# A vision tower on one core: narrow attention in units of three images, MLP branches by running sums, expert down weights loaded later

## The reference

```python
emb = patches @ W_proj + b_proj + pos                      # 64 x 36 x 192
h = layernorm(emb + attention(emb))                        # attn1: 12 heads of 64, causal
# attn2 and mlp; images 0..31 "large", images 32..63 "small"
a = attn(ln(h), 12 heads of 16)                            # small: sum over i of g[i] * attn with 12/(i+1) heads
x = h + a
mlp(x) = gelu(x @ w_fc1 + b_fc1) @ w_fc2 + b_fc2           # small: sum over i of g[i] * mlp that
                                                           # sees and keeps only 192/(i+1) channels
h = layernorm(h + x + mlp(ln(x)))
h = layernorm(h + attention(h))                            # attn3: 12 heads of 16, distance bias
h = layernorm(h + moe(h))                                  # a shared MLP, and 2 of 8 experts
```

## Time and profile before

| what | value |
|---|---|
| median of three timed runs | 917.89 us |
| profiled execution | 915.19 us, span 913.5 us |
| PE busy | 837.2 us (92%) |
| VectorE (DVE) busy | 545.0 us (60%) |
| ScalarE (ACT) busy | 455.0 us (50%) |
| GpSimd (POOL) busy | 403.9 us (44%) |
| mean granted TensorE clock | 0.978 of full speed |

### The profile page before, as it was taken

How to read it: one execution, slowest core, us unless ns; L and a number is a source line. 1 busy time by engine, 2 the same in 40 slices (tenths; PEclk the granted TensorE clock), 3 DMA queues, 4 the chain that set the end, 5 groups by cost and what they waited for, 6 DMA issues and landing times. The chain is left out here.

```text
span 913.5 us, 21005 instructions
## 1 busy us (share of the span) xinstructions
PE 837.2 (92%) x7607; PEld 755.2 (83%) x7607; DVE 545.0 (60%) x1460; ACT 455.0 (50%) x1132; POOL 403.9 (44%) x466
## 2 busy tenths in 40 slices
PE   5999999999998798997999988988979999999985
PEld 5998998899997577776999986777767898999885
DVE  1435655465666788885743325889885622666573
ACT  1235565556544487874344425777835211555440
POOL 3424444354454443332442206777761275344461
PEclk9999999999999999999999998999979999999998
DMA  9810111011110131215300002633200023333161
GB/s 298 268 37 25 29 37 36 26 31 36 32 42 2 28 60 26 37 19 150 46 1 1 1 1 63 139 67 48 62 9 1 19 80 99 81 103 102 58 195 39
DMA packets 103236, 55.56 MB, mean 61 GB/s; under 512 B 67200, under 2 KB 93936, under 8 KB 103136
## 3 DMA queue, kind: packets, MB, share of 16 engines
q1 hardware_dynamic: 98128, 43.43, 19.8%
q0 software_dynamic: 3792, 7.84, 2.5%
q10 hardware_dynamic: 1216, 2.95, 1.0%
HBM read 29.61 MB, written 13.97 MB: 48 GB/s over the span
## 5 line engine op out<-in xcount | busy, mean ns | idle before, releaser
L858 POOL TENSOR_TENSOR attn_prob<-attn_prob,attn_recip 100x432 f32<-100x432 f32 x64 | 58.6, 915 | 75.7 <-DVE attn_recip L1235 75.5
L377 POOL TENSOR_TENSOR attn_prob_x<-attn_prob,attn_recip 100x864 f32<-100x864 f32 x32 | 52.7, 1646 | 52.6 <-DVE attn_recip L686 52.6
L1751 POOL DMA_INDIRECT results<-moe_hid_shared x43 | 41.3, 960 | 55.2 <-ACT moe_hid_shared L1968 55.2
L1483 ACT ACTIVATE mlp_hid<-psum,columns 128x384 f32<-128x384 f32 x72 | 39.6, 582 | 48.9 <-PE psum L78 31.0
L987 PEld LDWEIGHTS psum<-attn_prob_t,attn_values 108*64 108x64 f32 x1024 | 39.2, 141 | 12.9 <-ACT attn_prob_t L1106 7.0
L2358 PE MATMUL psum<-embed_w_tok,embed_patches 128*128 128x192 f32 x216 | 40.3, 351 | 10.1 <-DMA embed_w_tok<-in_tok_w 5.7
L2358 PEld LDWEIGHTS psum<-embed_w_tok,embed_patches 128*128 128x128 f32 x216 | 38.9, 207 | 11.0 <-DMA embed_w_tok<-in_tok_w 5.7
L987 PE MATMUL psum<-attn_prob_t,attn_values 108*64 108x36 f32 x1024 | 41.4, 227 | 6.1 <-ACT attn_prob_t L1106 2.7
L960 PE MATMUL psum<-attn_keys_a,attn_q_a 128*64 128x288 f32 x256 | 46.2, 440 | 0.0
L1099 ACT ACTIVATE attn_prob<-attn_prob 100x432 f32<-100x432 f32 x64 | 36.6, 571 | 15.5 <-POOL attn_prob L865 15.0
L1365 POOL TENSOR_TENSOR mlp_rstd<-mlp_var_eps,neg_half 128x1 f32<-128x1 f32 x18 | 10.6, 590 | 75.1 <-DVE mlp_var_eps L1547 75.1
(11 more groups left out here) (462 smaller groups left out, 2851.0 us busy)
## 6 DMA issues: line engine op xcount, KB each, us to landing
embed_patches<-in_x SPq DMA_DIRECT2D x8, 768.0 KB, 24.6
sorted_rows<-mlp_pad_zeros SPq DMA_DIRECT2D x1, 4214.0 KB, 16.8
moe_hid_shared<-sorted_rows SPq DMA_DIRECT2D x43, 98.0 KB, 2.1
attn_v<-attn_v_tok SPq DMA_DIRECT2D x16, 216.0 KB
attn_values<-attn_v_tok SPq DMA_DIRECT2D x96, 27.0 KB
side_raw_a<-in_w_gu_dram SPq DMA_DIRECT2D x8, 288.0 KB, 3.2
side_raw_b<-in_w_gu_dram SPq DMA_DIRECT2D x16, 144.0 KB, 3.3
h_rows<-results SPq DMA_DIRECT2D x6, 288.0 KB, 5.3
```

The source lines that it names most:

```text
L377: nc.gpsimd.tensor_tensor(prob_x[k % 2][:, :, :, :], prob[k % 3][:, :, :].rearrange("p h (a n) -> p h a n", a=1) .to_broadcast([QP, HEADS, ...
L858: nc.gpsimd.tensor_tensor(pr, pr, recip[k % 2][:, :].rearrange("p (h a) -> p h a", a=1) .to_broadcast([QP, HEADS, SEQ]), ALU.mult).then_in ...
L1483: nc.scalar.activation(hid[(n // chunks) % 2][:, c, :], bank(n % 3)[:, 0:MW], ACT.Gelu, bias=b_up[:, c:c + 1]).then_inc(S["gelu_done"], 1)
L1751: nc.gpsimd.indirect_dma_start(out=results, out_offset=bass.IndirectOffsetOnAxis(ap=x_in[j % x_ring][:, D:D + 1].bitcast(U32), axis=0), in ...
```

## The change

Narrow attention: a group has 3 units, of 3, 3 and 2 images (24 steps and 3 to drain). q is laid out for each unit and image with zeros around its 36 columns, so that a slice of 108 columns has the image's own queries in its place and zeros elsewhere. The scores of a unit are 3 (or 2) matmuls a key block that add up in the same 108 rows of the bank. Every elementwise instruction on a unit has 108 rows instead of 100. GpSimd clears all of q at the start. ScalarE copies q in two instructions. The value products and their copies move into the last of the three steps, behind the masks, which are made 5 and 3. Splitting the low side weights moves to the first step of the next group.

MLP: the first layer's weights and x are kept in three pieces: channels 0 to 63 with high and low part of x stacked (`first`, 2 matmuls), 64 to 95 stacked (`mid`, 1 matmul), 96 to 191 (`last`, 3 matmuls). For small images a hidden chunk of the three branches is one sum in one bank: the piece `first`, gelu, `mid` added, gelu, `last` added, gelu. PE goes in steps of three chunks, `up_group(k)` and then `down_group(k - 1)`, k = 0 to 5, and the last down group of an iteration follows the next iteration's first up group. Large images take six matmuls a chunk. The x for the next iteration is made by VectorE from the bank, rounded by ScalarE and split by VectorE. `hid` and the normalised x share one buffer.

Experts: the four loads of down weights are issued at the start of the expert stage, and PE waits for them before the first down product.

PE near the end of a steady group in attn2: in before the last step of a group has scores, mix and then the values.

```diff
+UQ = 3 * SEQ
+NARROW_PER_GROUP = 3
+NARROW_UNITS = TOK // WIDE * NARROW_PER_GROUP
...
+def group_by_x(nc, out, w, cols, x, group):
+
+    pairs = (((w.first_hi, x.first), (w.first_lo, x.first)), ((w.mid, x.mid),),
+             ((w.last_hi, x.last_hi), (w.last_hi, x.last_lo), (w.last_lo, x.last_hi)))[group]
+    for n, (weights, toks) in enumerate(pairs):
+        last = nc.tensor.matmul(out, weights[:, cols], toks[:, :], start=(group == 0 and n == 0),
+                                stop=(group == 2 and n == 2), skip_group_check=True)
+    return last
...
+    def images(k):
+        return 3 if k % per_group < 2 else 2
+
+    def tokens_upto(count):
+        return count // per_group * WIDE + count % per_group * UQ
...
-    q_a = [sb(f"q_a{p}", [P, WIDE + 28]) for p in range(2)]
-    q_b = [sb(f"q_b{p}", [P, WIDE + 28]) for p in range(2)]
+    q_a = [sb(f"q_a{p}", [P, per_group, 3, block]) for p in range(2)]
+    q_b = [sb(f"q_b{p}", [P, per_group, 3, block]) for p in range(2)]
...
-            nc.gpsimd.memset(q_a[p][:, WIDE:], 0.0).then_inc(S["pads_cleared"], 1)
-            nc.gpsimd.memset(q_b[p][:, :], 0.0).then_inc(S["pads_cleared"], 1)
+            nc.gpsimd.memset(q_a[p][:, :, :, :], 0.0).then_inc(S["pads_cleared"], 1)
+            nc.gpsimd.memset(q_b[p][:, :, :, :], 0.0).then_inc(S["pads_cleared"], 1)
...
-            if side and j == 3 and g < side.steps:
-                side.split_b(pool, g)
+            if side and j == 0 and 1 <= g <= side.steps:
+                side.split_b(pool, g - 1)
...
             for q, keys, h0, h1 in ((q_a, keys_a, 0, 8), (q_b, keys_b, 8, HEADS)):
-                for a in range(2):
-                    at = u * UNIT + a * SEQ
-                    last = nc.tensor.matmul(ps[64 * a:64 * a + 64, h0:h1, :], q[g % 2][:, at:at + 64],
-                                            keys[g % 2][:, :, at:at + SEQ], start=True, stop=True)
+                for a in range(images(k)):
+                    at = u * UQ + a * SEQ
+                    last = nc.tensor.matmul(ps[0:UQ, h0:h1, :],
+                                            q[g % 2][:, u, :, :].rearrange("p a n -> p (a n)")[:, a * UQ:(a + 1) * UQ],
+                                            keys[g % 2][:, :, at:at + SEQ], start=(a == 0), stop=(a == images(k) - 1))
...
                 elif j == 1:
                     project(g, 0)
                     project(g, 1)
-                elif j == 2:
+                else:
                     project(g, 2)
-                else:
-                    for n in range(3):
-                        values(g, n)
             if 2 <= k < units + 2:
                 turn(k - 2)
             for t in ready_tiles(k):
                 project_out(t)
+            if g < groups and j == 2:
+                for n in range(3):
+                    values(g, n)
             if k == last + 2:
                 pe.wait_ge(S["v_copied"], 3 * groups)
                 following.turn(pe, S)
...
+            for us, count in ((slice(0, 2), 3), (slice(2, 3), 2)):
+                to = out[0:n, us, 0:count, 0:SEQ]
+                of = bank(0)[0:n, us.start * UQ:us.start * UQ + (us.stop - us.start) * count * SEQ].rearrange(
+                    "p (u a n) -> p u a n", a=count, n=SEQ)
+                if qk_bias is None:
+                    ins = nc.scalar.activation(to, of, ACT.Copy, scale=0.25)
+                else:
+                    ins = nc.scalar.activation(to, of, ACT.Identity, bias=qk_bias[0:n, c:c + 1], scale=0.25)
...
             if g < groups and j == 1:
-                mask_keys_a(g, range(4))
+                mask_keys_a(g, range(5))
             if g < groups and j == 2:
-                mask_keys_a(g, range(4, 8))
+                mask_keys_a(g, range(5, 8))
+                for n in range(3):
+                    copy_v(g, n)
             if k == last + 2:
...
+        def up_group(j, k):
+
+            for n in range(3 * k, 3 * k + 3):
+                pe.wait_ge(S["gelu_done"], before(1, j) + n - 2)
+                if n % 3 == 0 and n < 9:
+                    group_ready(share + j, group_of(n))
+                group_by_x(nc, bank(n % 3)[:, 0:MW], w_up, slice(chunk_of(n) * P, chunk_of(n) * P + P), xs,
+                           group_of(n)).then_inc(S["up_done"], 1)
+
+        def down_group(j, k):
+
+            i, final = share + j, k == 5
+            pe.wait_ge(S["gelu_done"], before(1, j) + 3 * k + 3)
+            if j == 0 and k == 0:
+                pe.wait_ge(S["down_scaled"], 5)
+            for t in range(3):
+                if k == 0:
+                    pe.wait_ge(S["mlp_added"], 3 * (i - 1) + t + 1)
+                for n in range(3 * k, 3 * k + 3):
+                    w = w_dn_wide if n == 0 else w_dn_s[2 - group_of(n)][:, chunk_of(n), :]
+                    last = nc.tensor.matmul(bank(3 + t)[:, 0:w.shape[1]], hid_step(n)[:, t * MT:(t + 1) * MT], w,
+                                            start=(n == 0), stop=(n == 17), skip_group_check=True)
                 if final:
                     last.then_inc(S["down_done"], 1)
...
+                if j > 0:
+                    up(j)
+                transpose_x(j + 1)
+                down(j)
+                return
+            for k in range(6):
+                up_group(j, k)
+                if k == 0 and j > 0:
+                    down_group(j - 1, 5)
+                elif 1 <= k < 5:
+                    down_group(j, k - 1)
             if following:
-                transpose_x(part * share + j + 1)
+                transpose_x(share + j + 1)
             else:
-                pe.wait_ge(S["x_split"], part * share + j)
                 after.turn(pe, S)
-            down(part, j, branches - 1)
+            down_group(j, 4)
+            if not following:
+                down_group(j, 5)
 
         for c in range(0, chunks, 2):
...
+            act.wait_ge(S["x_affine"], 2 * i - 1)
+            nc.scalar.activation(xs.first[0:DB, :], x_aff_a[0:DB, :], ACT.Copy).then_inc(S["x_rounded"], 1)
+            nc.scalar.activation(xs.mid[DB:TILE, :], x_aff_a[DB:TILE, :], ACT.Copy).then_inc(S["x_rounded"], 1)
+            nc.scalar.activation(xs.mid[0:32, :], x_aff_a[DB:TILE, :], ACT.Copy).then_inc(S["x_rounded"], 1)
+            act.wait_ge(S["x_affine"], 2 * i)
+            nc.scalar.activation(xs.last_hi[:, :], x_aff_b[:, :], ACT.Copy).then_inc(S["x_rounded"], 1)
...
+            for to, of in loads:
+                sp.dma_start(to, of).then_inc(S["down_loaded"], 16)
...
+                        pe.wait_ge(S["down_loaded"], 16 * len(loads))
```

364 lines of the change are left out of this document (226 added, 138 removed).

## The result

The changed kernel takes 951.87 us (median of 4, 949.21 to 953.85), the kernel before, run beside it, 918.00 (912.96 to 918.18). The ratio is 1.037, 95% interval [1.033, 1.042]. I had said 932 and slower by over 1%; the sign is right, the size is not: the change costs 2.4 times what I gave it (33.9 us for 14), and the time lies 7 us above my range.

A forecast was written before the change was run, and what follows sets the result against it. PE, busy 9 tenths or more almost everywhere, was taken as the bound, with waits mostly for VectorE in narrow attention. 915.2 + 26.1 (attention) - 9.9 (MLP) = 931.4, stated as 932 us; range 913 to 945.

The forecast's parts named there:

- six groups of attn2: Steady groups of eight images in attn2: period from 14.3 to 16.3 us each, +12.0 us for six.
- six groups of attn3: Steady groups of eight images in attn3: period from 15.1 to 17.5 us each, +14.4 us for six.
- first groups: First group of attn2 and attn3: no mix or turn for two steps, mix no longer before its values land; -1.0, -1.5.
- end of attn2, before the MLP: Last group of attn2: dependent steps, one step fewer but a longer scores step; +1 us.
- end of attn3: Last group of attn3: one step fewer in a stretch of 29.5 us partly at low clock; -2 us.
- MLP, small images: Up products as running sums, 36 matmuls instead of 66: net -4.35 us an iteration, three iterations -13.
- the serial scores: Narrow attention scores on PE: padded products cannot run side by side; 2.24 us a unit of three, +2.84 us a group.
- PE's floor: PE's own work in a steady narrow-attention group: from 12.8 to 15.2 us, padding added and saved turns and boundaries subtracted.
- It waits 1.1 us in attn2 and 2.3 in attn3: PE before a group's value products, waiting for ScalarE's last masks of keys a; bounds 0 and 3.5 us.
- A: Narrow attention: mask wait hidden, only PE's floor counts; attention 20.4 us less, 911 to 914 us; chance 0.22.
- B: Narrow attention scores: padded products still overlap two by two, 0.39 us an image; 907 us; chance 0.08.
- C: MLP: running sums don't pay, PE waits 0.5 us eighteen times for gelu or x's split, +9: 941; chance 0.10.

The follow-up runs named there:

- vector_masks: Changed kernel with all masks of keys a and keys b on VectorE, keys b ahead of the last step's scores: 962.31 us, 1.008 to the kernel before.
- padded_pairs: Old attention and new MLP, late loads, with queries padded with zeros in units of two images: 968.06 us, ratio 1.014 to the kernel before.
- changed_again: The changed kernel itself, run again later beside its variants: 988.88 us, ratio 1.035 to the kernel before.
- masks_early: Changed kernel with all eight masks of keys a on ScalarE in the middle step, keys b unmoved: 1000.33 us, ratio 1.048 to the kernel before.
- old_attention_new_mlp: Changed kernel with the narrow attention of the kernel before, keeping running sums and late down-weight loads: 946.68 us, ratio 0.992 to the kernel before.
- late_loads_alone: Kernel before with only the four down-weight loads moved to the start of the expert stage: 954.44 us beside 955.65, ratio 0.999.

## Why the prediction was right in sign and wrong in size

The forecast was +16.2 on the profiled execution, the measurement +38.6 of span. Term by term:

| term | forecast | measured |
|---|---|---|
| start of attn2, of attn3 | +1.6, +1.6 | +1.5, +0.8 |
| six groups of attn2 | +12.0 | +20.9 |
| six groups of attn3 | +14.4 | +19.4 |
| first groups | -1.0, -1.5 | +1.5, +2.3 |
| end of attn2, before the MLP | +1, and 1.05 of the large images' | +5.9 |
| end of attn3 | -2 | -2.9, and -0.7 behind it |
| MLP, small images | -13 | -14.2 |
| MLP, the other large images | +2.1 | +2.3 |
| down weights | 0 | 0 |
| (the embedding, not of the change) | | +1.8 |

**Right: the serial scores and PE's floor.** The first term held to 2%: 2.29 us a unit for 2.24. PE's own work in a group, from steps without a wait, is 3.98 + 4.91 + 4.94 + 2.25 output tiles of 0.67 = 15.3 us (15.2 forecast; the 4.94 is a last step of vector_masks without its tile), and padded_pairs shows that the padding does this by itself. The rule that the prediction takes from the Trainium skill (TensorEngine Tiling (Array Packing), its table of speedups), up to 2x for a stationary side of at most 64, was the right warning: 1.55 us a unit of two instead of 0.79.

**Failed: the step "It waits 1.1 us in attn2 and 2.3 in attn3".** That wait was the right one to look for, and for ScalarE's masks it was nearly right: PE's idle time before the first value product is 1.2 us a group in attn2 and 1.6 in attn3 (means of the six). The last mask comes 11.6 us into the last two steps in attn3 (11.4 forecast), and in attn2 at 10.1 as forecast in two groups and at 10.8 in four, as in the one shown, where ScalarE stands for the third projection; PE is later too in most groups. What failed is that I looked at keys a alone. In attn2 the second value product waits for VectorE's keys b, behind four other instructions, 0.5 us a group; in attn3 the output tile waits for ScalarE's copy of z, 0.4 us. Each wait also begins with the tail of a burst, some 0.15 us that the idle time leaves out. Together it is 17.8 - 15.3 - 0.5 = 2.0 us a group in attn2 for my 1.1 (the 0.5 is the next point), and 18.3 - 15.3 - 0.5 = 2.5 in attn3 for my 2.3. And the first groups have the same wait, where I had put a gain of 1.0 and 1.5: PE is idle there for 3.5 and 3.95 us, and they are 17.9 and 16.8 us long in changed_again, 15.5 and 12.9 with the masks on VectorE. masks_early shows that there are two chains, and vector_masks that without both the forecast's 16 us a group comes out.

Of the 22.4 us that the sum lacked, 8.9 are in the steady groups of attn2, 5.0 in those of attn3, 6.3 in the two first groups and 3.9 at the MLP's head; the rest gives back 1.7.

**Missing: the clock behind a wait.** In attn2 and attn3 of before it was 1.00 in every steady group, and I carried that over to a kernel with longer waits: PE's idle time in the six groups goes from 4.6 to 10.2 us and from 8.9 to 12.3, and its longest single piece from 1.4 to 1.8 and 2.6. It costs 1.5 to 1.8 us four times in the steady groups, 0.5 us a group on average. The sum had no term for it, that is, it put it at nothing.

**Missing: what the MLP change does to its own head.** I gave the end of attn2 +1. But the first block of the MLP is rounded in four copies and split in three instructions instead of two and two, on ScalarE and VectorE ahead of what the last steps of attn2 wait for, and behind the longer idle stretch the clock is low for longer (13.7 us instead of 3.4): +5.9. old_attention_new_mlp has it with the old attention.

**Luck: the end of attn3.** I gave it -2 for one step fewer and a low clock, and -2.9 was measured. But the same stretch, last group to last scores, takes 11.75 us in the kernel before, 10.4 in late_loads_alone and 9.05 in old_attention_new_mlp, all with the old attention, and 8.8 in the changed kernel. The clock is low in it for 6.8, 3.4, 0 and 0 us. So nearly all of the gain is the clock there, not the step, and no run shows what took the low clock away.

**Rivals.** A (the wait is hidden) is what vector_masks makes of the kernel, and there the ratio is 1.008. My 911 to 914 for it, a ratio under 1.00, was too low: 0.6 to 1.4 us a group of other waits stay, and the MLP's head was missing. B is dead by the 2.29 us, C by the MLP's timeline.

So the net of the change, by stretches of one profile each: padding about +20 us (by padded_pairs), units of three without mask waits -3 (vector_masks, in which VectorE makes the masks, has 120.0 and 121.8 us in the two stages, padded_pairs 121.4 and 123.3), the masks' place and its clock +26 to +27, the MLP -11.9 with +5.9 to +6.9 at its head, starts +2.3, attn3's end -2.9, loads 0.
